# Storing attention contexts unturned and normalising them in the output projection

## The chip, the cores and the metric

The kernel runs on one core of a Trainium2 chip. The metric is the device time of one execution in microseconds. The core has five engines with a queue each: PE (TensorE: matrix products, with weight loads, PEld, beside them), DVE (VectorE), ACT (ScalarE), POOL (GpSimd) and SP (SyncE, which issues most transfers). They meet only through semaphores, so the order in which each engine's work is written is the order in which it is done.

## The reference

```python
x = L0_attn_x                       # 16 sequences x 1024 tokens x 256
xn = layernorm(x)
q, k, v = (split_heads(xn @ W) for W in (W_q, W_k, W_v))   # 16 heads of 16
q, k = rope(q), rope(k)
scores = causal(q @ k.T)
ctx = softmax(scores / 4) @ v
s = ctx @ W_o
e = argmax(softmax(xn @ w_router.T))          # one of 8 experts for each token
h = xn @ w_fc[e].T
h = where(h >= 0, h, 0.5 * h) ** 2
out = x + s * silu(h @ w_proj[e].T)
```

## The kernel before, in words

There are four stages, one behind the other; between the last ones the engines meet at a block's end.

`project_phase` makes queries, keys and values of 32 tiles of 512 tokens and the table of places of the tokens, sorted by expert. The change doesn't touch it.

`attention_phase` works on 64 groups of four heads (16 sequences x 4). For each group three kinds of work stand on PE: *row items*, score tiles with queries on the partitions (L1044), of which DVE takes each query's maximum (L966); *columns*, the same scores with keys on the partitions and the maximum already subtracted by extra rows of the operand (L1118), of which ACT takes the exponential (L946); and *values* (L1081), the product of the values and the exponentials, which adds up in one PSUM bank `ps_ctx`. POOL sets the upper triangle of the diagonal tiles to zero (L912). The row items of a group are done while the columns of the group before it are. A group has 12 steps (`STEPS`): 4 for the first 512 queries (widths 512, 384, 256, 128) and 8 for the second (five of 512, then 384, 256, 128), each of 4 heads. `ORDER` is written out by hand: for each step and head it says which pieces of other work stand behind its columns on PE (R a row item, M a turning of maxima, X a turning of a context, V the values of an earlier step), and `ITEMS` gives the row items' order as (block of queries, head); a row item of block i has 128 x (i + 1) columns. Row items, maxima and contexts share four PSUM banks `ps_rows`, given out in turn by `place()`; a row item of more than 512 columns takes two.

The raw context of a half (512 queries) lies in `ps_ctx` with 32 partitions for a head: 16 of the context, one with the sum of the exponentials, the others unused. ACT copies it to `ctx_raw` (`copy_ctx`, L936), PE turns it, so that the queries stand on the partitions (`transpose_ctx`, L1068), ACT moves it to `ctx_T` (`move_ctx`, L929), DVE inverts the sums (`invert`, L1001), POOL multiplies (`normalise`, L892), and SP stores 64 columns of `ctx_dram` for each token (`store_ctx`, L811).

`expert_output_phase` has two parts. First 72 blocks of 256 sorted tokens pass through their expert: PE turns them (L1345), DVE copies (L1307), PE expands (L1356), ACT halves (L1269), DVE takes the maximum (L1313), ACT squares (L1276), PE contracts (L1366), ACT makes the gate (L1283), SP stores it; POOL copies the block's weights (L1249). Blocks overlap: in round n PE turns block n, expands n-1 and contracts n-2. SP also loads the contexts of 14 tiles and 6 tiles of x beforehand.

Then the output, tile by tile (32 of 512 tokens): POOL gathers the gates by token (L1258, four gathers a tile, two tiles ahead), PE turns the context (`turn_ctx`, L1370, two tiles ahead), ACT copies it to `cT` (L1299), PE multiplies by W_o (`project`, L1380), DVE multiplies by the gate (L1329) and adds x (L1334), and SP stores.

Of the kernel before, what the change touches and what calls it, by code (L numbers as in the profile page):

```python
# [27 lines left out]
P = 128  # L28
# [4 lines left out]
GH = 4  # L33
# [577 lines left out]
def attention_phase(nc, ctx, parts_dram, v_dram, ctx_dram, xn_dram, xs_dram, token_row, w_fc, w_proj, expert_in, first_in,  # L611
# [27 lines left out]
    ident_f, ident_b, mask = consts  # L639
# [7 lines left out]
    ctx_T = sb("ctx_T", [P, HALVES, IB * GH, VP])  # L647
    inv_sum = sb("inv_sum", [P, HALVES, IB * GH])
    ctx_out = sb("ctx_out", [P, HALVES, IB, GW])
# [14 lines left out]
    ctx_moved = sem("ctx_moved")  # L664
    normalised = sem("normalised")
# [7 lines left out]
    inv_ready = sem("inv_ready")  # L673
# [8 lines left out]
    for c in range(HALVES):  # L682
        for j in range(IB * (c + 1)):
# [6 lines left out]
    ITEMS = [(0, 2), (1, 0), (1, 1), (0, 3), (1, 2), (2, 0), (3, 2), (3, 0),  # L690
# [22 lines left out]
    def events():  # L713

        rows, maxima = iter(range(NI)), iter((1, 0))
        contexts, steps = iter((1, 0)), iter(range(-1, NS - 1))
        names = {"R": ("row", rows), "M": ("max", maxima), "X": ("ctx", contexts), "V": ("values", steps)}
# [3 lines left out]
    assert not any(x in "MX" for x in ORDER[-1][-1])  # L721
# [5 lines left out]
    def happens(what, n):  # L727
        return not (n == 0 and what in (("ctx", 1), ("values", -1)) or
                    n == N - 1 and (what[0] == "row" or what == ("max", 0)))

    def place():
# [3 lines left out]
               [[what for _, _, what in in_group(n)] for n in range(N)] + [[("ctx", 1)]]  # L735
        out, last, number = [], {}, 0
        left = {"row": 0, "max": 0, "ctx": 0}
        for whats in uses:
            pos, placed = 0, {}
            for what in whats:  # L740
# [3 lines left out]
                before = {"row": 0, "max": 0, "ctx": 0}  # L744
# [20 lines left out]

    INVERT_AFTER = 3

    def rows_before_inverse(n):

        out, rows, due = {}, 0, {}  # L770
        place_of = [(k, h) for k, h, _ in in_group(n)]
        for i, (k, h, what) in enumerate(in_group(n)):
            if what[0] == "row":
                rows += 1
            elif what[0] == "ctx":
                same = sum(1 for x, y in zip(place_of[i + 1:], in_group(n)[i + 1:]) if x == (k, h) and y[2][0] == "row")
                out[what] = min(rows + same + INVERT_AFTER, NI)
        return out
# [22 lines left out]
    def _(sp):  # L801
# [71 lines left out]
    def _(pool):  # L873
# [18 lines left out]
        def normalise(n, c):  # L892
            pool.wait_ge(inv_ready, 2 * n + c + 1)
            if n > 0:
                pool.wait_ge(ctx_stored[c], 16 * n)
            nc.gpsimd.tensor_tensor(ctx_out[:, c].rearrange("p i (h e) -> p (i h) e", h=GH), ctx_T[:, c, :, 0:HD],
                                    inv_sum[:, c, :].unsqueeze(2).broadcast_to((P, IB * GH, HD)),
                                    ALU.mult).then_inc(normalised, 1)

        def group(n, r, first, last):  # L900
            for k, (c, j, q0, w, diag_before, diag) in enumerate(STEPS):
                for k0, _, (what, arg) in in_group(n):
                    if what == "ctx" and k == min(k0 + 2, NS - 1):
                        normalise(n - arg, arg)
# [11 lines left out]
        normalise(N - 1, 1)  # L916
# [4 lines left out]
    def _(act):  # L921
# [7 lines left out]
        def move_ctx(n, c, slot, bank):  # L929
            act.wait_ge(slot_ready, slot + 1)  # L930
            if n > 0:
                act.wait_ge(normalised, 2 * (n - 1) + c + 1)
            nc.scalar.activation(ctx_T[:, c].rearrange("p i e -> p (i e)"),
                                 ps_rows[:, 512 * bank:512 * bank + IB * GH * VP], ACT.Copy).then_inc(ctx_moved, 1)

        def copy_ctx(n, c):  # L936
            act.wait_ge(pv_done, NS * n + HALF_END[c])
            nc.scalar.activation(ctx_raw[:, c, :], ps_ctx[:], ACT.Copy).then_inc(ctx_copied, 1)

        def group(n, r, first, last):  # L940
            for k, (c, j, q0, w, diag_before, diag) in enumerate(STEPS):
                if not (first and k < PB):
                    act.wait_ge(pv_done, NS * n + k - PB + 1)
                for h in range(GH):
# [7 lines left out]
                    for what, arg in moves_after(n, k, h):  # L952
                        slot, bank, _ = PLACES[n][what, arg]
                        if what == "max":
                            move_max(n + 1 - arg, arg, slot, bank)
                        else:
                            move_ctx(n - arg, arg, slot, bank)
# [4 lines left out]
        move_ctx(N - 1, 1, *PLACES[N]["ctx", 1][:2])  # L962

    @block.vector
    def _(dve):
# [35 lines left out]
        def invert(m, c):  # L1001
# [476 lines left out]
```

## Time and profile before

| | us |
|---|---|
| median of 3 runs (2407.6 to 2410.84) | 2410.21 |
| the profiled execution | 2409.12 |
| its span, from the first to the last instruction | 2407.4 |

| stage | from, to (us of the span) |
|---|---|
| projection | 0 to about 415 |
| attention | to 2049 |
| experts | 2054 to 2214 |
| output projection | to 2407 |

The page gives for each engine its busy time, its share of the span and the instructions. An engine that is busy all the time need not bound the kernel, since the records of matrix products overlap; the distance from the start of one instruction to the start of the next is the time that it takes from its engine when nothing waits.

### The profile page before, as it was taken

The page shows a single profiled execution, that of the slowest core. Times are in us where ns is not written, and L with a number is a line of the kernel's source. Part 1 is how long each engine was busy: PE and PEld are TensorE (multiplying, and loading weights), DVE is VectorE, ACT ScalarE, POOL GpSimd, SP SyncE. Part 2 cuts the span into 40 slices and gives each one's busy share as a digit, 9 for nine tenths or more (in the row PEclk, how much of TensorE's full clock was granted, in tenths as well). Part 3 has the DMA queues.
Part 4 walks back from the last instruction along what each step waited for, and adds up shares of the span by engine and source line. Part 5 has one row for each costly group of instructions (what it writes and reads, how often), then busy time and mean ns, then how long its engine had stood idle before and what let it go on. Part 6 is the DMA issues. An engine that isn't in the chain of part 4 may idle for free. (4 is left out here: it accounts for less than half of the span.)

```text
span 2407.4 us, 96050 instructions
## 1 busy us (share of the span) xinstructions
PE 2276.9 (95%) x38509; PEld 1342.8 (56%) x38509; DVE 2010.7 (84%) x5739; ACT 1787.7 (74%) x4319; POOL 1050.7 (44%) x1252
## 2 busy tenths in 40 slices
PE   7999994999999999999999999999999999899787
PEld 6777771544545445445454454444454544788676
DVE  7999998999999999999998999999999995454444
ACT  6777771888888888888888888888888888555111
POOL 6999995222223333333333333333332333223666
PEclk9999995999999999999999999999999999999998
DMA  6899885454533433434344334334333331796998
GB/s 215 287 300 301 299 271 164 155 181 164 168 106 99 133 101 103 129 96 128 107 126 130 107 107 127 96 110 124 105 112 111 105 100 30 261 322 246 326 333 262
DMA packets 302572, 406.28 MB, mean 169 GB/s; under 512 B 99248, under 2 KB 233648, under 8 KB 302000
## 3 DMA queue, kind: packets, MB, share of 16 engines
q1 hardware_dynamic: 289840, 366.58, 48.4%
q0 software_dynamic: 12288, 33.57, 4.1%
q8 instruction: 304, 4.98, 0.8%
q14 instruction: 140, 1.15, 0.1%
HBM read 225.46 MB, written 173.02 MB: 166 GB/s over the span
## 5 line engine op out<-in xcount | busy, mean ns | idle before, releaser
L976 DVE CUSTOM_DVE_ANT_0 dump<-ps_rows,mask 128x128 bf16<-128x128 f32 (+7 forms) x2048 | 1471.1, 753 | 132.8 <-issue 108.3
L946 ACT ACTIVATE probs<-ps_cols 128x512 f32<-128x512 f32 (+3 forms) x3072 | 1314.8, 499 | 242.8 <-PE ps_cols L1118 226.5
L1118 PE MATMUL ps_cols<-q_st,k_st 99*32 99x512 bf16 (+3 forms) x12288 | 864.2, 327 | 5.1 <-DMA q_st<-max_T 2.8
L1052 PE MATMUL ps_rows<-k_st,q_st 96*32 96x128 bf16 (+3 forms) x12288 | 817.9, 330 | 18.8 <-DVE row_max L976 7.6
L912 POOL TENSOR_SCALAR_AFFINE_SELECT probs<-probs 128x512 f32<-128x512 f32 x512 | 325.0, 635 | 1039.3 <-ACT probs L946 1034.8
L1094 PE MATMUL ps_ctx<-probs,v_st 128*32 128x512 f32 (+3 forms) x6144 | 633.2, 487 | 1.2 <-POOL probs L912 1.0
L1118 PEld LDWEIGHTS ps_cols<-q_st,k_st 99*32 99x32 bf16 x12288 | 322.1, 95 | 343.7 <-ACT probs L946 173.7
L1052 PEld LDWEIGHTS ps_rows<-k_st,q_st 96*32 96x32 bf16 x12288 | 287.8, 96 | 383.3 <-DVE row_max L976 237.8
L1094 PEld LDWEIGHTS ps_ctx<-probs,v_st 128*32 128x32 f32 x6144 | 168.5, 110 | 92.0 <-POOL probs L912 15.6
L976 DVE DVE_READ_ACCUMULATOR2_ANT row_max<- 128x1 f32 x2048 | 171.8, 84 | 0.0
L1388 PE MATMUL ps_t<-w_o_sb,cT 128*128 128x256 f32 x512 | 128.0, 408 | 31.2 <-DVE prod L1329 29.2
L1258 POOL DMA_INDIRECT gate<-g_dram,slot x128 | 128.5, 1004 | 63.4 <-issue 35.1
L321 POOL TENSOR_TENSOR rest<-roped,parts 128x1024 f32<-128x1024 f32 x64 | 138.2, 2160 | 25.7 <-ACT parts L372 21.1
L888 POOL DMA_INDIRECT xs_dram<-xn_sb,slot x128 | 125.8, 983 | 33.7 <-issue 33.4
L327 POOL TENSOR_TENSOR parts<-rest,parts 128x1024 bf16<-128x1024 f32 x64 | 139.7, 2183 | 0.0
L1299 ACT ACTIVATE cT<-ps_t 128x512 f32<-128x512 f32 x64 | 34.6, 596 | 137.3 <-PE ps_t L1376 137.3
L1329 DVE TENSOR_TENSOR prod<-ps_t,gate 128x512 f32<-128x512 f32 x64 | 41.3, 686 | 112.7 <-DMA gate<-g_dram,slot 112.6
L1388 PEld LDWEIGHTS ps_t<-w_o_sb,cT 128*128 128x128 f32 x512 | 102.6, 206 | 49.7 <-issue 27.6
L378 ACT ACTIVATE parts<-rest 128x1024 bf16<-128x1024 f32 x64 | 67.7, 1058 | 75.7 <-POOL rest L321 75.6
L560 PE MATMUL ps_qk<-xT_hi,w_all_hi 128*128 128x512 f32 x256 | 106.5, 416 | 0.0
L560 PE MATMUL ps_vr<-w_all_hi,xT_hi 128*128 128x264 f32 x256 | 78.3, 306 | 24.0 <-DVE xT_lo L434 23.4
L560 PE MATMUL ps_qk<-xT_hi,w_all_lo 128*128 128x512 f32 x256 | 100.9, 394 | 0.0
(115 smaller groups left out, 2556.5 us busy)
## 6 DMA issues: line engine op xcount, KB each, us to landing
parts_dram<-parts SPq DMA_DIRECT2D x64, 768.0 KB, 4.1
q_st<-parts_dram SPq DMA_DIRECT2D x384, 128.0 KB
k_st<-parts_dram SPq DMA_DIRECT2D x384, 128.0 KB
xs_dram<-zeros SPq DMA_DIRECT2D x36, 512.0 KB, 4.2
xs_sb<-xs_dram SPq DMA_DIRECT2D x72, 256.0 KB, 4.4
g_dram<-g_sb SPq DMA_DIRECT2D x72, 256.0 KB, 3.3
v_dram<-v_sb SPq DMA_DIRECT2D x32, 544.0 KB, 4.9
v_st<-v_dram SPq DMA_DIRECT2D x64, 272.0 KB
```

The lines of the kernel that those rows point to most:

```text
L321: nc.gpsimd.tensor_tensor(rest[:, m % 2], roped[:, m % 2].rearrange("p k t -> p (k t)"), parts[:, t % 2, a, 0], ALU.subtract).then_inc(res ...
L327: nc.gpsimd.tensor_tensor(parts[:, t % 2, a, 2], rest[:, m % 2], parts[:, t % 2, a, 1], ALU.subtract).then_inc(part3_done, 1)
L560: mm = nc.tensor.matmul(out, lhs(i, c), rhs(j, c), start=((c, i, j) == PASSES[0]), stop=((c, i, j) == PASSES[-1]))
L888: pool.indirect_dma_start(out=xs_dram[:, :], out_offset=bass.IndirectOffsetOnAxis(ap=token_row[:, s:s + 1], axis=0), in_=xn_sb[:, u, s % S ...
L912: nc.gpsimd.affine_select(out=tri, in_=tri, compare_op=ALU.is_ge, fill=0.0, base=0, pattern=[[0, GH], [1, P]], channel_multiplier=-1).then ...
L946: nc.scalar.activation(probs[:, k % PB, h, 0:w], ps_cols[(GH * k + h) % CB][:, 0:w], ACT.Exp).then_inc(exp_done, 1)
L976: nc.vector.tensor_tensor_reduce(out=dump[:, done % 2, 0:n], in0=ps_rows[:, 512 * bank:512 * bank + n], in1=mask[:, S - n:S], scale=1.0, s ...
L1052: mm = nc.tensor.matmul(ps_rows[a:a + VW, 512 * (bank + c):512 * (bank + c) + w], q_st[r][0:KS, i // IB, q0 + a:q0 + a + VW], k_st[r][0:KS ...
L1094: mm = nc.tensor.matmul(ps_ctx[VW * h:VW * (h + 1), o:o + w], v_st[r][:, j * V_ROW + VP * h:j * V_ROW + VP * h + VW], probs[:, k % PB, h, ...
L1118: mm = nc.tensor.matmul(ps_cols[(GH * k + h) % CB][a:a + VW, 0:w], k_st[r][:, j // IB, k0 + a:k0 + a + VW], q_st[r][:, c, h * 512 + q0 - 5 ...
L1258: pool.indirect_dma_start(out=gate[:, r, s, :], out_offset=None, in_=g_dram[:, :], in_offset=bass.IndirectOffsetOnAxis(ap=token_row[:, t * ...
L1388: mm = nc.tensor.matmul(ps_y[u][i][:, (s % 2) * D:(s % 2 + 1) * D], cT[:, u, c, s * P:(s + 1) * P], w_o_sb[:, c, :], start=(c == 0), stop= ...
```

## The change

The contexts are no longer turned. ACT's copy of `ps_ctx`, 128 partitions by 512 queries with the sums of the exponentials in it, is stored as it is. `ctx_dram` gets a new layout, (tile, group of heads, partition, token), and twice the size. In the attention `transpose_ctx`, `move_ctx`, `invert` and `normalise` go; ACT's copy waits for the store of the half before. `ITEMS` and `ORDER` are new; X is gone from the latter.

In the output, a tile's context is loaded as two transfers of 128 rows of 2 KB, already turned as `cT` needs it. The sums of all tiles (1 MB) are loaded once behind block 4 into the buffer that `cT` later uses. DVE inverts them and splits them into three bf16 parts, one operation a block in blocks 12 to 35 (4 sets of 6 operations of 128 x 512). POOL sets a table of zeros to ones where a row's head is a column's head. PE multiplies that table by the three parts (6 products of 512 columns a tile), which spreads the inverses over the 16 partitions of each head, and DVE multiplies the context by them into `cT` (2 operations of 128 x 512 a tile). ACT has no work there any more. The product with the gate is written over the gate.

```diff
-    ITEMS = [(0, 2), (1, 0), (1, 1), (0, 3), (1, 2), (2, 0), (3, 2), (3, 0),
-             (3, 3), (2, 3), (0, 0), (3, 1), (0, 1), (2, 1), (1, 3), (2, 2),
-             (6, 2), (7, 2), (5, 2), (6, 3), (5, 1), (7, 1), (6, 1), (7, 0),
-             (5, 0), (4, 3), (6, 0), (4, 1), (5, 3), (4, 2), (7, 3), (4, 0)]
+    ITEMS = [(2, 3), (0, 0), (1, 2), (0, 2), (1, 3), (1, 0), (3, 1), (3, 3),
+             (3, 2), (0, 3), (0, 1), (2, 1), (3, 0), (2, 0), (2, 2), (1, 1),
+             (4, 3), (4, 0), (7, 3), (5, 2), (6, 3), (5, 1), (7, 1), (6, 2),
+             (5, 3), (7, 2), (6, 1), (6, 0), (4, 2), (4, 1), (7, 0), (5, 0)]
...
-        ("R", "RR", "RR", "VR"),
-        ("", "RRM", "RV", "R"),
-        ("", "RRX", "RR", ""),
-        ("VR", "", "R", "R"),
-        ("", "", "RV", "V"),
-        ("", "R", "RV", "R"),
-        ("", "R", "", "RV"),
-        ("R", "", "R", "V"),
-        ("R", "", "X", "MR"),
-        ("", "V", "R", ""),
-        ("R", "VR", "", "R"),
+        ("R", "R", "RRV", "R"),
+        ("RR", "M", "RR", "V"),
+        ("RR", "", "RR", "R"),
+        ("R", "V", "", "R"),
+        ("V", "R", "", "RV"),
+        ("R", "", "RV", "R"),
+        ("", "R", "VM", ""),
+        ("R", "", "RV", "R"),
+        ("", "R", "", "R"),
+        ("V", "R", "", "R"),
+        ("V", "R", "", "R"),
         ("V", "", "", "RV"),
...
         def store_ctx(n, b, r, c):
-            sp.wait_ge(normalised, 2 * n + c + 1)
-            sp.dma_start(ctx_dram[b * TPB + c, :, :, r * GW:(r + 1) * GW], ctx_out[:, c]).then_inc(ctx_stored[c], 16)
+            sp.wait_ge(ctx_copied, 2 * n + c + 1)
+            sp.dma_start(ctx_dram[b * TPB + c, r], ctx_raw[:, c]).then_inc(ctx_stored[c], 16)
...
         def copy_ctx(n, c):
             act.wait_ge(pv_done, NS * n + HALF_END[c])
+            if n > 0:
+                act.wait_ge(ctx_stored[c], 16 * n)
             nc.scalar.activation(ctx_raw[:, c, :], ps_ctx[:], ACT.Copy).then_inc(ctx_copied, 1)
...
         def load_ctx(t):
-            sp.dma_start(c_sb[:, t % CR], ctx_dram[t]).then_inc(c_loaded[t % CR], 16)
+            rows = ctx_dram[t].rearrange("g (h e) t -> (g h) e t", h=GH)
+            for c in range(DC):
+                sp.dma_start(c_sb[:, t % CR, c], rows[c * H // DC:(c + 1) * H // DC, 0:HD]).then_inc(c_loaded[t % CR], 16)
+
+        def load_sums():
+
+            rows = ctx_dram.rearrange("(k i) g (h e) t -> (i g h) k e t", i=TS, h=GH)
+            sp.dma_start(sums, rows[:, :, HD]).then_inc(sums_loaded, 16)
...
     @block.gpsimd
     def _(pool):
+        nc.gpsimd.memset(choose_head[:], 0.0).then_inc(head_zeroed, 1)
         pool.wait_ge(weights_loaded, 16 * (DC + 1))
...
-        for t in range(NT):
-            for c in range(DC):
-                act.wait_ge(cT_ready, DC * t + c + 1)
-                if t >= 2:
-                    act.wait_ge(y_ready, 2 * (t - 1))
-                nc.scalar.activation(cT[:, t % 2, c, :], ps_cT[t % 2][c][:], ACT.Copy).then_inc(cT_copied, 1)
...
+        def invert(i):
+
+            k, step = divmod(i, INV_OPS)
+            inv, part = sums[:, k], inv_parts[:, :, k]
...
+            if step == 0:
+                nc.vector.reciprocal(inv, inv).then_inc(inverted, 1)
+            elif step in (1, 3, 5):
+                nc.vector.tensor_copy(part[:, step // 2], inv).then_inc(inverted, 1)
+            else:
+                nc.vector.tensor_tensor(inv, inv, part[:, step // 2 - 1], ALU.subtract).then_inc(inverted, 1)
+
+        def normalise(t):
+            for c in range(DC):
+                dve.wait_ge(c_loaded[t % CR], 16 * DC * (t // CR + 1))
+                dve.wait_ge(inv_ready, DC * t + c + 1)
+                if t >= 2:
+                    dve.wait_ge(y_ready, 2 * (t - 1))
+                nc.vector.tensor_tensor(cT[:, t % 2, c, :], c_sb[:, t % CR, c], ps_inv[t % 2][c][:],
+                                        ALU.mult).then_inc(cT_ready, 1)
...
+            if INVERT_AT <= n < INVERT_AT + INV_OPS * SETS:
+                invert(n - INVERT_AT)
+
+        normalise(0)
         for t in range(NT):
+            if t + 1 < NT:
+                normalise(t + 1)
...
-        def turn_ctx(t):
-            pe.wait_ge(c_loaded[t % CR], 16 * (t // CR + 1))
+        def spread_inverse(t):
+
+            k, i = divmod(t, TS)
             for c in range(DC):
                 if t >= 2:
-                    pe.wait_ge(cT_copied, DC * (t - 2) + c + 1)
-                for s in range(SUB):
-                    mm = nc.tensor.transpose(ps_cT[t % 2][c][:, s * P:(s + 1) * P],
-                                             c_sb[:, t % CR, s, c * P:(c + 1) * P], ident[:])
-                mm.then_inc(cT_ready, 1)
+                    pe.wait_ge(cT_ready, DC * (t - 2) + c + 1)
+                for part in range(PARTS):
+                    mm = nc.tensor.matmul(ps_inv[t % 2][c][:], choose_head[:, i * DC + c, :], inv_parts[:, part, k],
+                                          start=(part == 0), stop=(part == PARTS - 1))
+                mm.then_inc(inv_ready, 1)
```

## Rows read from the trace of the kernel before

**Rows 1.** The page: busy time by engine.
```profile
PE 2276.9 (95%) x38509; PEld 1342.8 (56%) x38509; DVE 2010.7 (84%) x5739; ACT 1787.7 (74%) x4319; POOL 1050.7 (44%) x1252
```
**Rows 2.** Windows: length, busy by engine (instructions), PE clock, DMA share, GB/s.
```profile
700.00:1000.00 300.00, 299.23 (x6488) 149.40 (x6484) 276.51 (x878) 257.25 (x640) 100.40 (x144) 1.00 0.38 113
2100.00:2200.00 100.00, 100.00 (x556) 86.47 (x554) 51.74 (x93) 59.41 (x140) 28.46 (x47) 1.00 0.94 326
2280.00:2300.00 20.00, 16.01 (x88) 13.97 (x87) 8.36 (x14) 4.34 (x8) 13.27 (x14) 1.00 1.04 370
```
**Rows 3.** Timeline of ACT: start, length, engine, line, what; idle before.
```profile
1003.95 2.07 ACT L946 ACTIVATE probs<-ps_cols 128x512 f32<-128x512 f32 x4 [0.47 <-PE ps_cols L1118]
```
**Rows 4.** Windows of the three thirds of one attention group.
```profile
1003.95:1011.52 7.57, 7.54 (x198) 4.17 (x190) 7.43 (x38) 6.56 (x19) 2.40 (x5) 1.00 0.40 116
1011.52:1021.40 9.88, 9.88 (x178) 4.30 (x173) 9.62 (x23) 8.88 (x17) 2.99 (x4) 1.00 0.69 202
1021.40:1029.20 7.80, 7.80 (x194) 4.11 (x190) 6.29 (x16) 6.20 (x18) 2.83 (x5) 1.00 0.06 15
```
**Rows 5.** Timeline of PE in the attention.
```profile
1000.03 1.03 PE L1094 MATMUL ps_ctx<-probs,v_st 128*32 128x512 f32 x8
1000.89 0.45 PE L1052 MATMUL ps_rows<-k_st,q_st 96*32 96x512 bf16 x8
...
1003.44 0.40 PE L1118 MATMUL ps_cols<-q_st,k_st 99*32 99x512 bf16 x4
1003.66 0.24 PE L1052 MATMUL ps_rows<-k_st,q_st 96*32 96x128 bf16 x4
...
1008.53 0.66 PE L1076 MATMUL ps_rows<-ident_f,ctx_raw 128*32 128x68 f32 x32
1009.01 0.29 PE L1118 MATMUL ps_cols<-q_st,k_st 99*32 99x256 bf16 x4
```
**Rows 6.** Waits in 700 to 1700 us: total, times, longest.
```profile
PEld ps_rows L1052 <- DVE row_max L976: 136.0, 456, 0.7
```
**Rows 7.** Timeline of DVE in the attention.
```profile
1002.24 1.22 DVE L976 CUSTOM_DVE_ANT_0 dump<-ps_rows,mask 128x1024 bf16<-128x1024 f32 x1
1003.38 0.08 DVE L976 DVE_READ_ACCUMULATOR2_ANT row_max<- 128x1 f32 x1
```
**Rows 8.** Tile `inv_sum`: count, min/median/max ns, first and last start.
```profile
L1005 DVE RECIPROCAL inv_sum<-ctx_T x128: 247/248/254, 442.9 to 2047.6; 128x16 f32<-128x16 f32 x128
```
**Rows 9.** Timeline of SP's issues in one group: start, length, what.
```profile
1017.57 0.58 SPq L813 DMA_DIRECT2D ctx_dram<-ctx_out  x1
```
**Rows 10.** Timeline of the seam between attention and experts.
```profile
2045.62 0.60 ACT L938 ACTIVATE ctx_raw<-ps_ctx 128x512 f32<-128x512 f32 x1 [1.31 <-PE ps_ctx L1094]
...
2048.62 0.52 SPq L813 DMA_DIRECT2D ctx_dram<-ctx_out  x1
2053.80 1.94 PE L1345 MATMUL ps_t<-ident_f,xs_sb 128*128 128x128 f32 x8 [6.64 <-PEq L1431]
2054.67 2.63 POOL L1249 COPY w_sb<-w_all 128x512 f32 x4 [6.08 <-issue]
```
**Rows 11.** Groups of POOL: count, busy us, mean ns, idle before.
```profile
L875 POOL MEMSET k_st<- 3x4096 bf16 x1 | 3.5, 3535 | 0.0
```
**Rows 12.** Timeline of DVE in the expert stage.
```profile
2103.31 0.43 DVE L1313 TENSOR_TENSOR leaky<-ps_t,halved 128x256 f32<-128x256 f32 x1 [0.59 <-ACT halved L1269]
...
2104.20 0.69 DVE L1307 COPY xsT<-ps_t 128x512 f32<-128x512 f32 x1 [0.46 <-PE ps_t L1345]
```
**Rows 13.** DVE's operations of 16 elements.
```profile
L992 DVE SCALAR_TENSOR_TENSOR max_rest<-row_max,max_parts 128x16 f32<-128x16 f32 x95 | 16.2, 171 | 0.0
```
**Rows 14.** The output stage: DVE's group, then a pair of tiles.
```profile
L1329 DVE TENSOR_TENSOR prod<-ps_t,gate 128x512 f32<-128x512 f32 x64 | 41.3, 686 | 112.7 <-DMA gate<-g_dram,slot 112.6
...
2285.01 1.29 DVE L1329 TENSOR_TENSOR prod<-ps_t,gate 128x512 f32<-128x512 f32 x2 [4.13 <-DMA gate<-g_dram,slot]
2289.09 1.29 DVE L1329 TENSOR_TENSOR prod<-ps_t,gate 128x512 f32<-128x512 f32 x2 [1.58 <-DMA gate<-g_dram,slot]
```

More of the change, by code:

```diff
@@ L715, in events @@
         rows, maxima = iter(range(NI)), iter((1, 0))
-        contexts, steps = iter((1, 0)), iter(range(-1, NS - 1))
-        names = {"R": ("row", rows), "M": ("max", maxima), "X": ("ctx", contexts), "V": ("values", steps)}
+        steps = iter(range(-1, NS - 1))
+        names = {"R": ("row", rows), "M": ("max", maxima), "V": ("values", steps)}
         return [(k, h, (names[x][0], next(names[x][1]))) for k in range(NS) for h in range(GH) for x in ORDER[k][h]]
     EVENTS = events()
-    assert not any(x in "MX" for x in ORDER[-1][-1])
+    assert "M" not in ORDER[-1][-1]
     def in_group(n):
@@ L727, in happens @@
     def happens(what, n):
-        return not (n == 0 and what in (("ctx", 1), ("values", -1)) or
+        return not (n == 0 and what == ("values", -1) or
                     n == N - 1 and (what[0] == "row" or what == ("max", 0)))
@@ L734, in place @@
         uses = [[("row", t) for t in range(NI)] + [("max", 0)]] + \
-               [[what for _, _, what in in_group(n)] for n in range(N)] + [[("ctx", 1)]]
+               [[what for _, _, what in in_group(n)] for n in range(N)]
         out, last, number = [], {}, 0
-        left = {"row": 0, "max": 0, "ctx": 0}
+        left = {"row": 0, "max": 0}
         for whats in uses:
@@ L743, in place @@
                 banks = [(pos + i) % RB for i in range(2 if wide else 1)]
-                before = {"row": 0, "max": 0, "ctx": 0}
+                before = {"row": 0, "max": 0}
                 for kind, count in [last[b] for b in banks if b in last]:
@@ L764, in moves_after @@
         return [what for kk, hh, what in in_group(n) if (kk, hh) == (k0, h0) and what[0] != "row"]
[L766 to L778, printed above, removed]
     assert (GH * NS) % CB == 0 and NS % PB == 0
@@ L952, in group @@
                     for what, arg in moves_after(n, k, h):
[L953 to L957, printed above, removed]
+                        move_max(n + 1 - arg, arg, *PLACES[n][what, arg][:2])
         move_max(0, 0, *FIRST_ROWS["max", 0][:2])
@@ L1012, in group @@
         def group(n, r, first, last):
-            inverses = rows_before_inverse(n)
             if last:
@@ L1023, in group @@
                         split_max(n + 1, 0, t - HALF_ITEMS)
-                    for (_, c), rows in inverses.items():
-                        if rows == t + 1:
-                            invert(n - c, c)
-            if last:
-                for _, c in inverses:
-                    invert(n - c, c)
         groups(dve, group)
-        invert(N - 1, 1)
     @block.tensor
@@ L1040, in banks_free @@
                 pe.wait_ge(max_moved, before["max"])
-            if before["ctx"]:
-                pe.wait_ge(ctx_moved, before["ctx"])
         def row_item(r, t, slot, bank, before):
@@ L1153, in expert_output_phase @@
     CR, XR = 14, 6
+    TS = P // H
+    SETS = NT // TS
+    SUMS_AT, INVERT_AT, INV_OPS = 4, 12, 6
     AHEAD = XR - 2
@@ L1170, in expert_output_phase @@
     cT = sb("cT", [P, 2, DC, TOK])
-    prod = sb("prod", [P, 2, W])
+    sums = cT[:].rearrange("p u c t -> p (u c) t")
     banks = [bank(f"ps_t{i}") for i in range(8)]
     ps_x, ps_h, ps_g = banks[0:2], banks[2:4], banks[4:6]
-    ps_cT = [banks[6:8], banks[0:2]]
+    ps_inv = [banks[6:8], banks[0:2]]
     ps_y = [banks[2:4], banks[4:6]]
```

84 lines of the change are left out of this document (31 added, 53 removed).

## The prediction

> **What bounds the kernel now.** The order of reading is: the page's busy times and slices, the busy time by stage, who waited for whom in the attention, one attention group instruction by instruction, then the seams and the two last stages.
>
> The page shows PE busy for 95% of the span and DVE for 84% [rows 1]. The slices show four stages: projection to about 415 us, attention to 2049, experts to 2214, output projection to the end. The change touches the last three. In the attention PE fills its windows and DVE is at 92% [rows 2]. One group lasts 25.25 us (first exponential at 1003.95, that of the next group at 1029.2). I cut it [rows 3] into steps 0 to 3, 4 to 7 and 8 to 11 at the starts of their first exponentials: 7.57, 9.88 and 7.80 us [rows 4].
>
> "Busy" of PE hides gaps because its ends are modelled, so I sum what PE must stream, by distances between starts [rows 5]. A bf16 product of 512 columns with its four column quarters side by side takes 0.22 us (1003.44 to 1003.66), taken as 0.213. An f32 product of 512 columns for four heads takes 0.86 (1000.03 to 1000.89), that is 4 x 0.213 and little else. The twelve steps have widths that sum to 4608 columns. Score columns: 4 heads x 4608 columns = 7.68 us. Score rows: the same, 7.68. Values: 7.68. Turning a context: 0.48 (1008.53 to 1009.01), twice a group 0.96. Turning maxima: about 0.1, twice 0.2. The sum is 24.20 of 25.25 us: PE streams 96% of the group, and 1.05 us a group is unfilled. That remainder is above all PE's loads waiting for DVE's row maxima [rows 6].
>
> DVE in the group, by distances between starts [rows 7]: 1.14 us for 1024 columns (1002.24 to 1003.38), and in the same stretch down to 0.215 for 128, with 0.34, 0.48, 0.61, 0.745, 0.88 and 1.01 for the widths between. Eight widths sum to 5.42, four heads 21.7, the chains of the maxima 0.7, two reciprocals about 0.4 (0.25 each [rows 8], less what overlaps): 22.8 of 25.25. DVE is the runner-up, 1.4 us behind PE's sum. ACT has idle time before most steps.
>
> **The change, part by part.**
>
> Attention, PE. Two turns of a context per group go: -0.96. The work left streams 23.24 us. The unfilled 1.05 us stays, if the new table of places feeds PE as evenly as the old. This is what I check by thirds, with the durations above, for both tables:
> - before, steps 0 to 3: PE 6.93, DVE 8.13, took 7.57 (0.64 over PE); steps 4 to 7: PE 9.60, DVE 8.08, took 9.88 (0.28 over); steps 8 to 11: PE 7.67, DVE 6.55, took 7.80 (0.13 over).
> - after: steps 0 to 3: PE 6.08, DVE 6.92; steps 4 to 7: PE 9.80, DVE 8.77; steps 8 to 11: PE 7.36, DVE 6.67.
>
> DVE outweighs PE only in the first third, by 1.20 before and 0.84 after. I scale the excess: 0.64 x 0.84 / 1.20 = 0.45. In the other thirds DVE's cover shrinks (1.5 to 1.0, 1.1 to 0.7), and steps 7 and 8 together ask 5.18 of DVE beside 4.48 of PE; I allow 0.35 and 0.2 there. New group: 23.24 + 1.0 = 24.25 us, 1.0 less. There are 63 groups with rows of the next group in them: **-63 us**. Bounds: if PE's unfilled time falls to 0.5, the group is 23.75 (-95); if DVE is what the group goes by, only DVE's own 0.39 leaves (-25).
>
> Attention, the others. ACT loses two moves a group, POOL two multiplications, DVE two reciprocals of 0.25 [rows 8]. POOL is busy for a third of the stage [rows 2] and ACT is idle in each third of the group [rows 4]; both count nothing, and with their cover gone they would still count nothing, because nothing is added to them. DVE's 0.39 is in the sums above. Added wait: ACT's copy of a raw context now waits for the store of the one a group earlier. ACT's next exponentials stand behind it, and PE's score columns wait for those. The store of a second half is issued at 1017.57, behind the operand loads [rows 9], and in this trace such a store lands in about 3 us; the next copy of a second half comes with the next group's first step, after 1029.2, 8 us later. A first half has as much. I take 0: the wait ends early from both sides, and nothing can be gained by it. SP's store moves no later, since it no longer waits for POOL, and carries 256 KB in rows of 2 KB in place of 128 KB in rows of 256 bytes, at a DMA share of 0.38 in this stage [rows 2]: 0.
>
> Last group: its two turns go, ACT and the masks set its pace; -1, between 0 and -2.
>
> **Tail of the attention.** Copy at 2045.62, turn 2046.36, move 2047.21, reciprocal 2047.63, multiplication 2047.97, store 2048.62, first expert matmul 2053.80 [rows 10]. Afterwards the store follows the copy, at 2046.22: **-2.4**. SP issues eight loads of expert rows, 3.9 us, ahead of the last store; they wait for the store of the first half, which is ready early in this group now, so they don't stand in its way; if they did, -0.9.
>
> **Start of the expert stage.** POOL first clears the 0/1 table, 2048 bf16 elements a partition. The nearest row is 3.5 us for 4096 [rows 11]: half, 1.8 us. Its copy of the first weights (2054.67) ends 0.4 us before PE needs it (2055.67) [rows 10], so about **+1.5** (0 if POOL gets there early, 1.9 at most). The selection at block 12 lies in POOL's slack (28% busy) [rows 2].
>
> **Expert stage, DVE.** It is 2.167 us a block and PE is full. DVE's copy runs 2104.20 to 2104.89 and feeds the expansion that starts 2.167 after the one at 2103.99, at 2106.16: slack 1.27. The new chain of the inverses starts when the leaky maximum ends, 2103.74 [rows 12]. A copy or subtraction of 512 elements costs at most 0.69, ends 2104.43, and makes the copy 0.23 late: nothing. There are 20 of these. The four reciprocals of 512 elements are not in the trace. The nearest row has 16 elements: 0.248 against 0.171 of other operations of 16 [rows 8, 13]. If the difference is per element, 77 / 16 = 4.8 ns, plus 1.04 (0.69 for 512 against 0.43 for 256 [rows 12]): 512 x 5.85 + 160 = 3.15 us. If it is fixed, 0.77. I take 3.15, since a difference between operations of one shape is rather per element. Then the reciprocal ends at 2106.89, the copy at 2107.58, and the expansion is 1.42 late: 4 x 1.42 = **+6** (0 from below). The load of the sums, 1 MB, comes at block 4 with expert rows loaded eight blocks (17 us) ahead: nothing; 3 us at most at the rate of these windows [rows 2].
>
> The Trainium skill, "VectorE: DVE Perf Modes", section "Walkthrough: the 8-slice pipeline in each mode", says that a reciprocal runs an iterative divide with a repeat count of 8. By it a reciprocal of 512 elements would be estimated at 160 + 8 x 532 = 4.4 us, the late time 2.7, and this term +11 in place of +6; by the same rule 16 elements would take 0.29, and the row shows 0.248, so the trace lies a little under it.
>
> **Output projection.** The loop is: gates land, DVE multiplies, POOL issues the next four gathers, they land; two tiles per 11.6 us (2273.4 to 2285.0) [rows 14], and the transfers are at 100% of the engines in this stretch [rows 2]. Removed: eight f32 turns of PE (1.04) and two ACT copies (1.08) a tile. Added: six bf16 matmuls of 512 columns (6 x 0.22 = 1.3) on PE, and two multiplications of PSUM on DVE, 0.69 each, 64 in all, 44 us of DVE. DVE needs 1.29 + 1.28 + 1.38 = 3.95 us a tile; gates land 4.1 us apart in the pair shown and 6 on the mean, and DVE has 112.7 us of waiting for them [rows 14]. The multiplication for tile t+1 is queued ahead of the product of t, behind the addition of t-1, so it falls in that wait. PE's spreading for t+2 waits for DVE's multiplication for t, with the projection of t+1 queued behind; both are ready before the gates of t land. SP issues two loads a tile in place of one, about 1 us more of a queue that is busy for 2 of 6 us. Bytes are the same. I take **0**; cover gone, +44 (all of it in the loop). Below: the bytes stay, so no gain over 3 us.
>
> **Sum.** Span 2407.4 - 63 - 1 - 2.4 + 1.5 + 6 = 2348.5. The profiled execution took 2409.12, 1.7 outside the span: 2350.2. The median of the runs shown is 1.1 above it: **2351 us**.
>
> **The rivals.**
> - *DVE becomes the bound of the attention.* For: it is at 92%, the new table asks more of DVE than of PE in steps 2 and 8 (2.00 against 1.07, 2.15 against 1.65), and only four PSUM banks lie between them. Against: over any third but the first PE has more to do. Gain 25 in place of 63: 2389.
> - *The new table fits better than the old.* For: the old one asked 8.87 of DVE from step 11 to step 3 with PE at 8.5, the new one 7.8 beside 7.7. The group falls to 23.75, -95 in place of -63: 2319. Against: DVE's margin to PE's sum shrinks from 1.4 to 0.9 us.
> - *DVE holds the end on both sides: slower.* In the output stage the 64 multiplications stand in the loop from landing to next gather (+44), and the attention goes by DVE (-25): 2351 + 44 + 38 = 2433. It decides once gates land closer together than DVE's 3.95 us a tile. For: 2285.01 to 2289.09 is 4.08. Against: the mean is 6, and DVE waits 112.7 us for gates, over twice the 44.
> - *Half of that,* delays in the output stage only when gates come in pairs: +20, 2371.
>
> **Chances.** Forecast 0.60, better table 0.14, DVE in the attention 0.12, pairs 0.09, slower 0.05. The range runs from the better table to just short of DVE in the attention: 2318 to 2387. A measurement of this kernel tells 0.2% (5 us) from no change. Faster 0.94, within 0.02, slower 0.04.
>
> **What would show it.** Attention group: distance between first exponentials 24.25 us (23.75 and 24.85 for the rivals), with PE's load still waiting for row maxima. From the last copy to the first expert matmul 2.4 us less. Reciprocals in the expert stage near 3.15 us, each with a late expansion. In the output stage, products still waiting for gates, and the stage still about 193 us. The forecast is wrong if the group falls by less than 0.5 us, or if the output stage grows by over 10.

## The result, and the profile after

The changed kernel takes 2381.76 us (median of 4 runs, 2380.38 to 2384.27) beside 2408.9 for the kernel before: the ratio is 0.9895, 95% interval 0.9869 to 0.9922. It is 27 us faster, clear of the measurement's uncertainty, and less than half of the 58 us that I forecast. The profiled execution's span is 2380.6 us against 2407.4.

The page of the changed kernel, busy time by engine, answers to [rows 1]:

```profile
PE 2243.9 (94%) x34337; PEld 1250.7 (53%) x34349; DVE 2041.1 (86%) x5699; ACT 1729.4 (73%) x4127; POOL 972.1 (41%) x1126
```

The whole says little about where the time went. Four places in the timelines cut the span into pieces that can be laid side by side: ACT's last copy of a context, PE's first turn in the expert stage, POOL's first gather of gates, and the end. In the changed kernel the first two are these rows of the timeline (start, length, engine, line):

```profile
1994.01 0.60 ACT L901 ACTIVATE ctx_raw<-ps_ctx 128x512 f32<-128x512 f32 x1 [1.31 <-PE ps_ctx L1023]
...
1997.16 1.94 PE L1319 MATMUL ps_t<-ident_f,xs_sb 128*128 128x128 f32 x8 [3.22 <-PEq L1408]
```

and, from the chain of waits (start, length, engine, what, line):

```profile
2175.62 1.02 POOL gate L1210
```

In the kernel before they stand at 2045.62, 2053.80 [rows 10] and 2217.70. The second trace of each kernel, taken later, gives the same lengths within 2 us.

| piece | before | after | difference | forecast |
|---|---|---|---|---|
| to the last copy | 2045.6 | 1994.0 | -51.6 | -64 |
| last copy to first turn | 8.2 | 3.2 | -5.0 | -2.4 |
| experts, to the first gather | 163.9 | 178.5 | +14.6 | +7.5 |
| output projection | 189.7 | 205.0 | +15.3 | 0 |
| sum | 2407.4 | 2380.6 | -26.8 | -58.9 |

Attention first. The group that begins last starts at 2021.53 before and 1970.47 after, 62 groups behind one at 445.60 and 446.17: 25.42 and 24.59 us a group, 0.83 less where I had 1.0. The windows and waits after, in the same columns as [rows 2] and [rows 6] (busy by engine in the order PE, PEld, DVE, ACT, POOL):

```profile
700.00:1000.00 300.00, 299.36 (x5904) 138.38 (x5900) 280.30 (x877) 259.97 (x633) 90.04 (x126) 1.00 0.42 127
```

```profile
PEld ps_rows L994 <- DVE row_max L934: 169.6, 579, 0.7
PEld ps_cols L1047 <- ACT probs L909: 157.5, 626, 0.4
```

PE is as full as before, and its loads still wait for maxima. The thirds of one group, cut as in [rows 4]:

```profile
1012.17:1019.02 6.85, 6.85 (x162) 3.30 (x154) 6.77 (x35) 6.15 (x19) 2.16 (x4) 1.00 0.10 28
1019.02:1029.05 10.03, 10.03 (x186) 4.37 (x182) 8.87 (x25) 9.09 (x19) 3.54 (x4) 1.00 0.78 235
1029.05:1036.68 7.63, 7.63 (x160) 3.71 (x156) 7.30 (x15) 6.03 (x17) 2.29 (x4) 1.00 0.32 111
```

In the first third DVE is busy for 6.77 of 6.85 us. The seam is where the store of 2 KB rows, issued right behind the copy, lets PE start after 3.2 us.

Then the two places where time came back. In the output stage the waits of the changed kernel are others than before (waiter, awaited: total, times, longest):

```profile
DVE gate L1303 <- DMA gate<-g_dram,slot: 42.9, 21, 6.7
DVE r_sb L1308 <- DMA r_sb<-in_x_dram: 42.4, 11, 4.5
POOL gate L1210 <- DVE gate L1303: 40.9, 25, 3.5
```

DVE now waits 42.4 us for x, which it never did before, and POOL waits 40.9 us for DVE's product, 17.5 before. So DVE is late because x is late, and the gathers are late in turn. Why x is late stands on SP's queue:

```profile
2236.19 5.64 SPq L1144 DMA_DIRECT2D c_sb<-ctx_dram  x2
2241.87 0.66 SPq L1177 DMA_DIRECT2D out_dram<-r_sb  x1
2242.58 2.06 SPq L1152 DMA_DIRECT2D r_sb<-in_x_dram  x1
2244.68 6.16 SPq L1144 DMA_DIRECT2D c_sb<-ctx_dram  x2
```

The two issues of a tile's context hold SP for 5 to 6 us, and SP has no pause between one tile's 8 to 9 us and the next. Before, one issue took about 1 us:

```profile
2246.94 1.01 SPq L1207 DMA_DIRECT2D c_sb<-ctx_dram  x1
2250.21 0.38 SPq L1233 DMA_DIRECT2D out_dram<-r_sb  x1
2250.63 0.51 SPq L1210 DMA_DIRECT2D r_sb<-in_x_dram  x1
```

Those rows are from the second trace of the kernel before. The transfers themselves slowed down. The same 50 us window of the second trace of the kernel before and of that of the changed one (last two columns: mean busy share of the 16 transfer engines, GB/s):

```profile
2240.00:2290.00 50.00, 41.20 (x207) 35.17 (x205) 19.91 (x32) 9.23 (x18) 33.70 (x34) 0.93 1.00 339
```

```profile
2240.00:2290.00 50.00, 35.92 (x145) 25.37 (x144) 24.36 (x40) 0.00 (x0) 26.03 (x29) 0.93 0.93 272
```

There is always a transfer waiting on SP, and yet the engines are busy for 93% on the mean and move 272 GB/s where they moved 339. The windows lie at different places of the two output stages; over the whole stages it is 276 GB/s in place of 299. PE's clock is no part of it: the mean granted clock over the output stage is 0.93 in both traces. Three theories were put to the test. **A:** the load of a context names its rows as 8 heads of 16, and a transfer whose outermost count is 8 is carried by only part of the 16 engines. **B:** rows of 2 KB in place of 4 KB, two loads in place of one. **C:** DVE's 64 multiplications stand in the loop.

### The profile page after: what moved, and what is told of

It is laid out like the page before. It is cut to its first block and busy times, and to the rows that moved or that the text cites. A ratio compares the mean times of both kernels' runs of the same rounds, so it can differ in the third digit from the quotient of the medians.

```text
span 2380.6 us, 86989 instructions
## 1 busy us (share of the span) xinstructions
PE 2243.9 (94%) x34337; PEld 1250.7 (53%) x34349; DVE 2041.1 (86%) x5699; ACT 1729.4 (73%) x4127; POOL 972.1 (41%) x1126
## 5 line engine op out<-in xcount | busy, mean ns | idle before, releaser
L934 DVE CUSTOM_DVE_ANT_0 dump<-ps_rows,mask 128x384 bf16<-128x384 f32 (+7 forms) x2048 | 1462.7, 755 | 108.9 <-issue 95.7
L1047 PE MATMUL ps_cols<-q_st,k_st 99*32 99x512 bf16 (+3 forms) x12288 | 881.0, 328 | 5.9 <-DMA q_st<-max_T 3.1
L994 PE MATMUL ps_rows<-k_st,q_st 96*32 96x384 bf16 (+3 forms) x12288 | 823.5, 331 | 15.4 <-DVE row_max L934 7.6
L1047 PEld LDWEIGHTS ps_cols<-q_st,k_st 99*32 99x32 bf16 x12288 | 316.6, 95 | 402.2 <-ACT probs L909 258.6
L994 PEld LDWEIGHTS ps_rows<-k_st,q_st 96*32 96x32 bf16 x12288 | 280.7, 95 | 377.0 <-DVE row_max L934 281.0
L1210 POOL DMA_INDIRECT gate<-g_dram,slot x128 | 123.8, 967 | 82.8 <-DVE gate L1303 40.9
L560 PE MATMUL ps_vr<-w_all_hi,xT_hi 128*128 128x264 f32 x256 | 78.2, 305 | 24.5 <-DVE xT_lo L434 23.8
L560 PE MATMUL ps_qk<-xT_lo,w_all_hi 128*128 128x512 f32 x256 | 100.7, 393 | 0.0
L1252 DVE COPY xsT<-ps_t 128x512 f32<-128x512 f32 x72 | 49.4, 686 | 51.2 <-PE ps_t L1319 50.2
```

Source lines behind the costliest of these rows:

```text
L560: mm = nc.tensor.matmul(out, lhs(i, c), rhs(j, c), start=((c, i, j) == PASSES[0]), stop=((c, i, j) == PASSES[-1]))
L934: nc.vector.tensor_tensor_reduce(out=dump[:, done % 2, 0:n], in0=ps_rows[:, 512 * bank:512 * bank + n], in1=mask[:, S - n:S], scale=1.0, s ...
L994: mm = nc.tensor.matmul(ps_rows[a:a + VW, 512 * (bank + c):512 * (bank + c) + w], q_st[r][0:KS, i // IB, q0 + a:q0 + a + VW], k_st[r][0:KS ...
L1047: mm = nc.tensor.matmul(ps_cols[(GH * k + h) % CB][a:a + VW, 0:w], k_st[r][:, j // IB, k0 + a:k0 + a + VW], q_st[r][:, c, h * 512 + q0 - 5 ...
L1210: pool.indirect_dma_start(out=gate[:, r, s, :], out_offset=None, in_=g_dram[:, :], in_offset=bass.IndirectOffsetOnAxis(ap=token_row[:, t * ...
```

## The experiments

The first four runs came from a chip on which the kernel before takes 2554 us, and the last one from another on which it takes 2551. On both, DVE, ACT and PE's loads pause for 1 to 2 us at one place of most attention groups, and the output stages of some kernels are longer too. No trace of the kernel before was kept there. These five runs are compared only among themselves; the other runs stand beside 2410 us.

**Rows first.** The same rows, the same bytes, named the other way round; the rows of W_o and the 0/1 table follow.

```diff
-                sp.dma_start(c_sb[:, t % CR, c], rows[c * H // DC:(c + 1) * H // DC, 0:HD]).then_inc(c_loaded[t % CR], 16)
+                sp.dma_start(c_sb[:, t % CR, c], rows[c * H // DC:(c + 1) * H // DC, 0:HD].rearrange("h e t -> e h t")).then_inc(c_loaded[t % CR], 16)
...
-                sp.dma_start(w_o_sb[:], w_o.rearrange("(c p) n -> p c n", p=P)).then_inc(wo_loaded, 16)
+                for c in range(DC):
+                    sp.dma_start(w_o_sb[:, c], w_o[c * P:(c + 1) * P].rearrange("(h e) n -> e h n", e=HD)).then_inc(wo_loaded, 16)
...
-                                        pattern=[[-H // DC, TS * DC], [-1, H // DC], [0, HD]],
+                                        pattern=[[-H // DC, TS * DC], [0, HD], [-1, H // DC]],
```

> The changed kernel with the 128 rows of each context load named as 16 rows of 8 heads instead of 8 heads of 16 rows; the rows of W_o and the 0/1 table are permuted to match, bytes and row length are the same. Theory A (a load whose outermost count is 8 is carried by only part of the 16 transfer engines, so the load is slow and clogs SP's queue): issues of context loads in the output stage fall from 2.8 us each to about 0.6, the output stage falls from 205 us to about 190 and the expert stage from 178.5 to about 170; whole 2358 us. Theory B (rows of 2 KB in place of 4 KB, two loads a tile in place of one): nothing changes, 2381. Theory C (DVE's 64 multiplications stand in the loop): nothing changes, 2381.

**Flat loads.**

```diff
-                sp.dma_start(c_sb[:, t % CR, c], rows[c * H // DC:(c + 1) * H // DC, 0:HD]).then_inc(c_loaded[t % CR], 16)
+                sp.dma_start(c_sb[:, t % CR, c], ctx_dram[t, c]).then_inc(c_loaded[t % CR], 16)
```

> The changed kernel, but each context load takes 128 rows that lie one behind the other (a whole group of four heads) in place of 8 heads of 16 rows; row length, number of loads and bytes are the same, and what is multiplied by W_o is not the context any more. Theory A: as the run with the rows first, 2358 us. A variant of it, that what counts is how the rows lie in memory (16 rows, a gap of 16) and not the outermost count: this one is fast and the run with rows first slow. Theories B and C: 2381.

**The kernel before, by heads.**

```diff
-            sp.dma_start(c_sb[:, t % CR], ctx_dram[t]).then_inc(c_loaded[t % CR], 16)
+            rows = ctx_dram[t].rearrange("p s d -> (p s d)").rearrange("(h e t) -> h e t", h=H // DC, e=2 * HD)
+            half = c_sb[:, t % CR].rearrange("p s d -> p (s d)")
+            for c in range(DC):
+                sp.dma_start(half[:, c * TOK:(c + 1) * TOK], rows[:, c * HD:(c + 1) * HD]).then_inc(c_loaded[t % CR], 16)
```

> The kernel before with one thing of the change: each context load is cut into two of 8 outer pieces of 16 rows of 2 KB (the same bytes in a different order, so the result of the output projection is not the reference's). Theory A: the output stage grows from 190 to about 205 us and the expert stage from 164 to about 172, whole about 2432 us. Theory B gives the same here. Theory C: 2410, unchanged, since DVE has no multiplication of contexts here.

**Old places.** ITEMS and ORDER of the kernel before, with the X struck out of ORDER, in the changed kernel.

> The changed kernel with the table of places of before (ITEMS and ORDER), the turns of contexts struck out of it. It tells what the new table is worth. If a group is PE's stream plus a fixed unfilled time, the old table gives as much as the new one: group 24.5 us, whole 2382. If DVE's lag in the first third decides (8.13 us of DVE beside 6.4 of PE without the turn), the group stays near 24.9 and the whole is about 2405.

| run | ratio to before (95%) | experts | output |
|---|---|---|---|
| old places (both last stages as in the change) | 1.0154 (1.0137, 1.0171) | 178.2 | 219.2 |
| rows first | 0.9871 (0.983, 0.9911) | 172.0 | 204.8 |
| flat loads | 0.9903 (0.9874, 0.9931) | 172.4 | 201.9 |
| before, by heads | 1.0061 (1.0044, 1.0079) | 170.3 | 205.1 |

Against the old-places run, whose last two stages are those of the change, naming the rows first takes 6 us from the experts and 14 from the output, with two loads of 2 KB rows a tile all the same; the flat load takes 6 and 17. B and C both wanted no change and fall for this part. That the rows lie with gaps in memory costs little: rows first has the gaps, flat has not, and they differ by 3 us in the output. "Before, by heads" decides nothing here: without a trace of the kernel before on this chip, its 205.1 has nothing to stand beside. The whole times mean nothing beside my expected 2358, which was for a chip without the pauses.

**Changed kernel, and before, again.**

> The changed kernel as it is, so that its stages stand beside those of the kernel before and of the experiments on the same chip. Theory A and C alike: ratio to before about 0.99, expert stage 178 us, output stage 205 to 220.

> The kernel before as it is, for its trace on the same chip. Ratio 1.00, expert stage 164 us, output stage 190 to 205.

2380.69 us, ratio 0.9876 (0.9855, 0.9897); experts 178.2, output 205.8. Before: 2406.36, ratio 0.9991 (0.9977, 1.0004); experts 163.9, output 188.3. The pieces repeat.

**Quarter inverses.** Rows first, and the reciprocals cut.

```diff
-            if step == 0:
-                nc.vector.reciprocal(inv, inv).then_inc(inverted, 1)
+            if step < 4:
+                piece = inv[:, step * P:(step + 1) * P]
+                nc.vector.reciprocal(piece, piece).then_inc(inverted, 1)
...
```

> The changed kernel with the rows first in the context loads, and each of the four reciprocals of 512 elements cut into four of 128 in four blocks. By the size of the reciprocal (3.34 us, each makes one expansion 1.27 us late) the expert stage falls by about 5 us against the run with the rows first (172 to 167). If what is left there comes from transfers alone, it stays at 172. The output stage stays as with the rows first; the whole is about 25 us under the changed kernel.

2353.09 us, ratio 0.9759 (0.9738, 0.978): it beats both kernels, the changed one by 27.6 us measured beside it. Experts 165.8 us, output 189.8. Its waits for x in the output stage and its window, the same 50 us:

```profile
DVE r_sb L1310 <- DMA r_sb<-in_x_dram: 2.8, 2, 1.5
```

```profile
2240.00:2290.00 50.00, 42.13 (x186) 30.34 (x187) 30.79 (x51) 0.00 (x0) 33.61 (x34) 1.00 1.07 314
```

The wait for x is gone, from 42 us to 3, and the engines are busy throughout. SP's issues are still long (2249.69, 5.34 us for two), so a long issue alone is no loss: it is how SP shows that the transfers are behind. Rows first without the quarters was not run on this chip, so the 189.8 is for both edits together; the quarters lie in the expert stage.

That this run ends 2 us from my forecast of 2351 confirms nothing. Its attention is 12 us longer than forecast; its tail is 3 us and its expert stage, with the quarters, 6 us shorter.

**Narrow multiplications.**

```diff
-                nc.vector.tensor_tensor(cT[:, t % 2, c, :], c_sb[:, t % CR, c], ps_inv[t % 2][c][:],
+                nc.vector.tensor_tensor(cT[:, t % 2, c, 0:1], c_sb[:, t % CR, c, 0:1], ps_inv[t % 2][c][:, 0:1],
```

> The rows first in the context loads, and DVE's 64 multiplications of contexts are made on 1 column in place of 512 (the rest of the result is left out), all waits kept. Theory C (DVE's multiplications stand in the output loop): the output stage falls by 20 to 40 us against the run with the rows first. Theory A alone: it falls by less than 5 us, since gates land 6 us apart and DVE needs 3.95 us.

2357.61 us, 0.9781 (0.9757, 0.9804); output 187.9 us against 189.8 with the full ones, and 188.3 to 189.7 before. DVE is busy for 83.7 us of this stage in place of 115.6, and 32 us less of its work brought 2 us: theory C falls. This run has whole reciprocals and rows first, so its experts (172.6) say what each is worth: 178.2 to 172.6 for the loads, 172.6 to 165.8 for the reciprocals.

**Narrow maxima.** The four row items of 1024 columns are looked at over 512.

```diff
+            seen = 512 if n == S else n
...
-            nc.vector.tensor_tensor_reduce(out=dump[:, done % 2, 0:n], in0=ps_rows[:, 512 * bank:512 * bank + n],
-                                           in1=mask[:, S - n:S],
+            nc.vector.tensor_tensor_reduce(out=dump[:, done % 2, 0:seen], in0=ps_rows[:, 512 * bank:512 * bank + seen],
+                                           in1=mask[:, S - n:S - n + seen],
```

> The changed kernel, but DVE takes the maximum of the four row items of 1024 columns a group over their first 512 columns only (part of the maxima is left out); PE still makes all their columns. DVE loses 4 x 0.53 = 2.1 us a group, PE nothing. If PE's unfilled time (24.52 us a group against a stream of 23.24) is waiting for DVE's maxima, the group falls to 23.9 or less. If it is waiting for ACT's exponentials or PE's own gaps, it stays above 24.3.

2379.49 us, 0.9875 (0.9855, 0.9895), as long as the changed kernel. DVE's busy time falls, the group doesn't:

```profile
700.00:1000.00 300.00, 299.35 (x5898) 139.90 (x5890) 258.84 (x877) 260.12 (x634) 89.08 (x125) 1.00 0.42 127
```

280.3 to 258.8 us of 300 on DVE, 299.4 on PE as before. The group is 24.56 us on the mean. PE's loads wait less for maxima in the same 1000 us, 109.6 us in place of 169.6, and nothing is gained:

```profile
PEld ps_rows L995 <- DVE row_max L935: 109.6, 381, 0.7
```

But the run doesn't touch the whole group. The items of 1024 columns all stand in steps 4 to 11. The first and the last third of one group:

```profile
1010.29:1017.14 6.85, 6.84 (x162) 3.30 (x154) 6.78 (x35) 6.15 (x18) 2.17 (x4) 1.00 0.10 26
1027.18:1034.81 7.63, 7.63 (x160) 3.73 (x156) 6.40 (x15) 6.02 (x17) 2.29 (x4) 1.00 0.28 90
```

The last third has 0.9 us less of DVE's work than in the changed kernel and takes the same 7.63 us; so does the middle one, 10.04 us with 0.8 less. In steps 4 to 11, then, DVE doesn't set the group, and its maxima are waited for in time in which PE still streams. In the first third DVE has as much to do as before, 6.78 of 6.85 us. That it sets the pace there isn't excluded by this run or any other.

**Old places, again.** The edit as above.

> The changed kernel with the table of places of before, turns struck out, a second time, since the first ran where the groups of every kernel took over 27 us. There the old table cost 0.95 us a group against the new one. If that is the table's own: group about 25.4 us here, as long as before although 0.96 us of PE's turns are gone, and the whole about 2435. If the fixed unfilled time of my forecast held for any table: group 24.3.

2455.7 us, 1.0192 (1.0175, 1.0209); 50 groups in the middle of the stage take 25.72 us each, against 24.57 with the new table and 25.42 in the kernel before, counted alike. PE is no longer full:

```profile
700.00:1000.00 300.00, 293.29 (x5662) 136.50 (x5658) 271.75 (x849) 247.89 (x609) 86.67 (x122) 1.00 0.39 120
```

The first third of a group, which took 7.57 us in the kernel before [rows 4], takes 7.94; the others take 9.86 and 7.83 as before:

```profile
1062.83:1070.77 7.94, 7.61 (x166) 3.64 (x162) 7.60 (x39) 6.27 (x18) 2.84 (x5) 1.00 0.17 55
```

The turns alone, taken out of the old table, make the group longer, and all of that in the first third. The new table is worth 1.15 us a group, 72 us in all, and without it the change is a loss of 46 us.

**Before, by heads, again.**

> The kernel before with each context load cut into two of 8 outer pieces of 16 rows of 2 KB, a second time beside kernels whose stages are known. Theory A: expert stage 164 to about 170 us, output stage 188 to about 205, whole about 2430. If the loads by heads only cost beside DVE's multiplications, the output stage stays at 190.

2430.57 us, 1.0087 (1.007, 1.0103), that is 21 us slower; experts 169.8 (163.9), output 204.8 (188.3 and 189.7). The one edit puts into the kernel before the +6 and the +15 to 16 that the loads cost in the change, with no multiplication of contexts on DVE. Alone it can't tell A from B, since it also halves the rows; rows first has the halved rows too and excludes B. Theory A stands from both sides.

**Narrow exponentials.** On the second of the chips with the pauses.

```diff
+        nc.gpsimd.memset(probs[:], 0.0).then_inc(probs_set, 1)
...
-                    nc.scalar.activation(probs[:, k % PB, h, 0:w], ps_cols[(GH * k + h) % CB][:, 0:w],
+                    w0 = min(w, 384)
+                    nc.scalar.activation(probs[:, k % PB, h, 0:w0], ps_cols[(GH * k + h) % CB][:, 0:w0],
```

> The changed kernel, but ACT takes the exponentials of the 512-column steps over their first 384 columns only (the rest is left out and stands as zero); PE and DVE do all their work. ACT loses 24 x 0.11 = 2.6 us a group. If PE waits for ACT's exponentials in what is left between its stream of 23.24 us and the group of 24.52, the group falls to about 24.0 or less. If PE's own time between pieces makes it up, it stays at 24.5.

2530.71 us, 0.9923 (0.99, 0.9945). The mean of 50 groups is 27.27 us against 27.41 in the rows-first run on the first, so 2.6 us less of ACT's work brought next to nothing. The short groups, which the pauses miss, take 24.37 and 24.51, 0.14 less. It points the same way as the narrow maxima, but the pauses and the two chips make it a weak witness.

## Why the prediction was wrong

**The step that failed** is the sentence on the output projection "Bytes are the same. I take **0**"; the expert stage has no term at all for the context loads that run in it. The output grew by 15.3 us, past the 10 that I had named as a sign of being wrong. The bytes were the same; how the load names its rows was not. I had seen that transfers are at 100% in this stretch [rows 2] and priced only their size and the number of issues. Runs from both sides give the price: naming the rows first takes 16 us from the output (205.8 to 189.8) and 5.6 from the experts (178.2 to 172.6); naming them by heads in the kernel before adds 15 to 16.5 and 5.9. As the waits show it, the mechanism goes: a context load is slow, transfers pile up, SP is held at its next issue, x comes late, DVE's addition waits, the next product and the next gather wait. In the expert stage it is the store of the gates that lands late, and ACT waits for its slot (8.8 us in the second trace, none before).

The Trainium skill, "DMA: Bandwidth & Descriptors", section "Why a DMA increments its semaphore by 16 and not by 1", says that a transfer uses the largest number of engines up to 16 that divides the slowest dimension's size on both sides. By it 8 heads give 8 engines and 16 rows of 8 give 16. The runs agree in sign and place. The traces don't name the engine of a packet, but they have the start and the duration of each, so one can count how many packets are under way at once. In a stretch of 150 to 160 us of the output stage it is exactly eight for 7% of the time in both kernels that load by heads (the changed one, 2180 to 2340 us, 7.3%; the kernel before by heads, 7.0%), and seven for 0.1 and 0.3%. In the kernel before, the flat loads and the quarter inverses it is eight for 0.8, 0.5 and 0.2%. So there are times at which exactly eight have work, which is what a load carried by eight of the sixteen would leave behind. I had not weighed that rule before the result.

**The attention** was right in its direction and a fifth too large. The group fell by 0.83 us against 1.0, -51.6 in place of -64. The term at fault is the first third: I scaled the excess over PE's sum there to 0.45 us, for a third of 6.53, and it took 6.85, an excess of 0.77. The other thirds came out at 10.03 and 7.63 where I had 10.15 and 7.56. In steps 4 to 11 the 1.7 us less of DVE's work a group (21.5 of 300 us, 12 groups) changed nothing, so what is unfilled there, about 0.5 us, is not waiting for maxima, as I had put it from [rows 6]. Part of it may be PE's own time, 512 columns taking 0.215 to 0.22 us and not 0.213, which over the 17.16 us of their stream would be an estimated 0.2 to 0.6 us; this is argued only. In the first third DVE is busy for 99% of the time, and by my own sums it has 6.92 us of work beside 6.08 of PE's. That DVE sets the pace there is likely and not shown, since no run took work from it in those steps.

**"If the new table feeds PE as evenly as the old"** hid more than it said. The old table with its turns struck out costs 25.72 us a group, 1.4 more than my rule of stream plus remainder gives. A table is fitted to one set of work, and the same gaps don't stay when a piece is taken out. Its excess is in the first third, where my count has 8.13 us of DVE's work beside 6.4 of PE's and the third takes 7.94; that fits DVE as the bound of that third. Why it takes 0.4 us more than before with less to do was not tried.

**The tail** gained 5.0 us where I had 2.4: the five hops of the old chain went as reckoned, and the last store, in rows of 2 KB and with no loads of expert rows ahead of it, lets PE in 2.5 us after its issue where it took 5.2.

**The start of the experts** was right in kind and 1 us too large: POOL clears the table in 1.80 us, and PE waits 0.53 us for the weights instead of the 1.5 that I gave it.

```profile
1997.12 1.80 POOL L1188 MEMSET choose_head<- 128x2048 bf16 x1 [3.66 <-POOLq L1408]
...
1999.63 2.05 PE L1330 MATMUL ps_t<-xsT,w_sb 128*128 128x256 f32 x4 [0.53 <-POOL w_sb L1194]
```

**The reciprocals** were right. Estimated 3.15 us and 1.42 us late each; in the trace 3.34, and the expansion behind the last is at 2076.14, 3.60 after the one before in place of 2.17, so 1.43 late:

```profile
L1270 DVE RECIPROCAL cT<-cT x4: 3341/3342/3343, 2028.6 to 2072.2; 128x512 f32<-128x512 f32 x4
```

```profile
2072.54 1.03 PE L1330 MATMUL ps_t<-xsT,w_sb 128*128 128x256 f32 x4
...
2076.14 1.13 PE L1330 MATMUL ps_t<-xsT,w_sb 128*128 128x256 f32 x4 [1.27 <-DVE xsT L1252]
```

4 x 1.43 = 5.7 of the +14.6; cutting them brought 6.8. With the 5.6 of the loads and 0.6 at the start, about 2 of the 14.6 us stay unexplained; even the quarter inverses end this stage 1.9 us later than the kernel before. Extrapolating the excess over a plain operation per element from 16 elements to 512 was within 6%. The repeat count of 8 of the Trainium skill, "VectorE: DVE Perf Modes", section "Walkthrough: the 8-slice pipeline in each mode", gave an estimate of 4.4 us; the measurement decides for less. With quarters of 128 elements in the next row, a further element costs (3.342 - 0.943) / 384 = 6.2 ns.

```profile
L1272 DVE RECIPROCAL cT<-cT x16: 941/943/945, 2026.9 to 2092.3; 128x128 f32<-128x128 f32 x16
```

**DVE in the output stage** was right: 32 of its 44 us taken away brought 2. The rival that ended slower and the one of "pairs" named the right stage for a wrong reason. Without the load's form the forecast's zero comes out, 189.8 us against 188.3 to 189.7.

## What to carry to other kernels

When a transfer is rewritten, compare how many rows its outermost dimension names on the side of memory, not only its bytes and the length of its rows; where the transfers are full, an outermost count of 8 cost 22 us here for 16 MB, and naming the same rows the other way round gave it back. A table of places must be judged for the work it carries: in the attention the same removal was worth -52 us with a new table and +18 with the old one. A wait of the weight loader or a runner-up at 93% need be no bound over a whole group and may still be one in a part of it; take 2 us of its work away and see, in the part that it is thought to bound.

## What the runs showed of the hardware that was not expected

- On two chips the kernel before takes 2554 and 2551 us in place of 2410. In the rows-first run the groups take 24.5 to 25.2 us up to 670 us of the span and over 25.9 from there on; the attention ends 150 us later than on a chip without this, and the output stage is 15 us longer. The pause comes at one place of the group, at the copy of the first half: DVE stops, ACT 0.3 us later, then PE's loads. The profile has no reason for DVE's wait ("issue") or for ACT's ("remote"), and the cause was not looked for. This is the timeline of that run:

```profile
1005.60 0.40 PE L1047 MATMUL ps_cols<-q_st,k_st 99*32 99x512 bf16 x2 [0.30 <-issue]
1006.45 0.60 ACT L901 ACTIVATE ctx_raw<-ps_ctx 128x512 f32<-128x512 f32 x1 [1.87 <-remote]
1006.45 0.82 DVE L934 CUSTOM_DVE_ANT_0 dump<-ps_rows,mask 128x640 bf16<-128x640 f32 x1 [2.15 <-issue]
```

- An issue of a context load on SP's queue takes 0.6 us at the median and up to 4.6 when transfers are behind (5.3 with the quarter inverses), and holds whatever stands behind it.
- DVE's copy of 512 elements to bf16 between buffers in SBUF takes 0.42 us, against 0.69 for one out of PSUM.
